# A two-layer decoder kernel: the second layer's VectorE roundings run one chain after the other, its next group's turns move up, and self attention's rough products are spread out

## What is computed

```
x = _layernorm(x + _L0_attn_ref(...))                 # a recurrence over 1024 steps
x = _layernorm(x + _L0_xattn_ref(x, ctx, ctx, mask0, ...))
x = _layernorm(x + _L0_ffn_ref(...))
x = _layernorm(x + _L1_attn_ref(x, W_qkv, W_out))     # 16 heads of 64, 1024 x 1024 scores
x = _layernorm(x + _L1_xattn_ref(x, ctx, ctx, mask1, ...))   # 16 heads of 16, 77 context rows
x = _layernorm(x + _L1_ffn_ref(x, w_gate, w_up, w_down))
```

```
scale = jnp.maximum(jnp.max(jnp.abs(xb), axis=-1, keepdims=True) / 6.0, 1e-12)
q = _GRID[jnp.searchsorted(_MID, jnp.abs(xb / scale))] * jnp.sign(xb) * scale
gate = fp4_linear(x, w_gate); y = fp4_linear(x, w_up)
h = jax.nn.silu(gate) * y                             # 704 wide
return fp4_linear(h, w_down)
```

## Time and profile before

| | |
|---|---|
| time, median of 3 runs | 2963.14 us (2959.21 to 2965.66) |
| the profiled execution | 2964.39 us |
| its span, first to last instruction | 2962.7 us |
| PE, DVE, ACT, POOL busy | 2087.9, 2176.3, 1751.9, 654.3 us |
| self attention's loops | about 1653 to 2500 us of the span |
| second layer | about 2515 us to the end |

### The profile page before, as it was taken

The page is one execution under the profiler, slowest core; times in us unless marked ns, Lnnn a source line. Parts: engine busy times, 40 slices in busy tenths (PEclk is TensorE's granted clock), DMA queues, the critical chain, the costliest instruction groups (busy, mean ns, idle before and its releaser), DMA issues. The chain is left out here.

```text
span 2962.7 us, 41501 instructions
## 1 busy us (share of the span) xinstructions
PE 2087.9 (70%) x11052; PEld 1171.3 (40%) x11052; DVE 2176.3 (73%) x10063; ACT 1751.9 (59%) x5698; POOL 654.3 (22%) x343
## 2 busy tenths in 40 slices
PE   6233655556455564655566899999999998888986
PEld 3122443344343443443344333333333333555553
DVE  5899999999999999999984455555555553276557
ACT  3678888888888888888841344444444443222231
POOL 0000000000000000000001366666666666000000
PEclk9555555565555655555555899999999998899898
DMA  5632223222223222222200000000000000210100
GB/s 124 140 94 61 55 48 66 53 52 67 48 52 67 51 53 66 53 49 65 53 4 4 4 13 17 16 7 16 16 11 12 16 11 20 73 37 14 43 8 8
DMA packets 86798, 123.55 MB, mean 42 GB/s; under 512 B 17444, under 2 KB 65224, under 8 KB 86600
## 3 DMA queue, kind: packets, MB, share of 16 engines
q1 hardware_dynamic: 86600, 121.37, 17.1%
HBM read 100.33 MB, written 21.00 MB: 41 GB/s over the span
## 5 line engine op out<-in xcount | busy, mean ns | idle before, releaser
L1505 ACT ACTIVATE mix_cand<-mix_pre,mixer_cbuf 128x32 f32<-128x32 f32 x2048 | 592.8, 289 | 167.8 <-DVE mix_pre L1435 83.6
L1502 ACT ACTIVATE mix_cand<-mix_state,mixer_cbuf 128x32 f32<-128x32 f32 x2048 | 652.7, 319 | 34.9 <-DVE mix_state L1427 4.7
L1936 DVE TENSOR_REDUCE self_tops<-self_rough 128x2 f32<-128x1024 f32 x256 | 311.7, 1217 | 411.6 <-PE self_rough L1708 411.6
L1422 DVE SCALAR_TENSOR_TENSOR mix_prod<-mixer_keys,mixer_cbuf,mix_cand 128x65 f32<-128x65 f32 x2048 | 582.1, 284 | 34.2 <-ACT mix_cand L1505 27.1
L1435 DVE SCALAR_TENSOR_TENSOR mix_pre<-mixer_keys,mix_gap,mix_state 128x32 f32<-128x32 f32 x2048 | 525.8, 257 | 27.8
L1427 DVE SCALAR_TENSOR_TENSOR mix_state<-mix_cand,mixer_cbuf 128x32 f32<-128x32 f32 x2048 | 506.9, 247 | 0.1
L1534 PE MATMUL mix_out<-all_ident,mix_state 128*128 128x128 f32 x512 | 162.0, 417 | 486.3 <-ACT mix_flat L1486 430.6
L1922 POOL TENSOR_TENSOR self_psum<-self_psum,self_prob 128x1024 f32<-128x1024 f32 x192 | 451.3, 2350 | 160.4 <-ACT self_prob L1849 151.1
L1849 ACT ACTIVATE self_prob<-self_sco 128x1024 f32<-128x1024 f32 x256 | 261.5, 1024 | 118.9 <-PE self_sco L1721 108.2
L886 POOL TENSOR_TENSOR mix_st_norm_rstd<-mix_st_norm_var,mix_half 128x2 f32<-128x2 f32 x24 | 16.7, 697 | 1318.1 <-DVE mix_st_norm_var L879 1318.1
L1534 PEld LDWEIGHTS mix_out<-all_ident,mix_state 128*128 128x128 f32 x512 | 82.6, 207 | 568.6 <-ACT mix_flat L1486 502.6
(11 more groups left out here) (386 smaller groups left out, 3257.7 us busy)
## 6 DMA issues: line engine op xcount, KB each, us to landing
mixer_keys<-k_rows SPq DMA_DIRECT2D x256, 260.0 KB, 4.9
aT_rows<-self_aT SPq DMA_DIRECT2D x32, 256.0 KB, 2.3
...
```

The lines of the kernel that those rows point to most:

```text
L1422: dve.scalar_tensor_tensor(prod[:, b, :], keys[:, h, b, s_, :], coef(NIB, h, s_, b), cand[:, b, s % 2, :], ALU.mult, ALU.mult, accum_out=g ...
L1502: act.activation(cand[:, b, (s + 1) % 2, NS:2 * NS], state[:, hp, sp_, b, :], ACT.Copy, scale=cbuf[:, h, KEEP, b, s_:s_ + 1]).then_inc(kep ...
L1505: act.activation(cand[:, b, (s + 1) % 2, 0:NS], pre[b], ACT.Tanh, scale=cbuf[:, h, BETA, b, s_:s_ + 1]).then_inc(c_ready[b], 1)
L1936: dve.tensor_reduce(tops[:, kh, t, :], rough[:, :, :], AX.X, ALU.max).then_inc(rough_taken, 1)
```

## The change

It has three parts. None removes a computation, and no buffer is added.

1. **Self attention.** The pieces of `rough_scores` move. Before, pieces 0 and 1, 3 and 4, and 5 and 6 each had only one `scores` between them. Now at least one larger product, or two `scores`, stands between two pieces, but for pieces 0 and 1, which have one `scores` and an `attend`. VectorE's first inversion stands before top 5 instead of behind it.
2. **Second layer, VectorE.** `lagging` is gone. Each norm and each rounding of a chain runs to its end before the other chain's begins, and `hidden_dve` is called for each tile: one's tile 0, two's norm1, two's tile 0, one's tile 1, two's tile 1. Only the last norm is still split, around the tops of the next group.
3. **Second layer, TensorE and ScalarE.** Both `flip1` of the next group stand before the down product of chain one's second tile, behind a new wait for chain two's `h_ready` (its bank 6 must have been read); both `queries_pe` and the first rough scores of the next group stand before chain two's second down product. The scores of chain one's first half of heads are split around chain two's rough scores. ScalarE copies both chains' turned tops before the first exponentials.

```
@@ self attention, TensorE @@
                     scores(hp, b, hf, 1)
-                    if more:
-                        rough_scores(hp + 1, of, to, 1)
                     if behind:
                         attend(hp - 1, b if hf else other, 3)
                     if more:
-                        rough_scores(hp + 1, of, to, 2)
+                        rough_scores(hp + 1, of, to, 1)
...
                         keys_queries(fills, "Q1" if hf else "K0", other)
+                    if more:
+                        rough_scores(hp + 1, of, to, 2)
                     scores(hp, b, hf, 2)
+                    scores(hp, b, hf, 3)
                     if more:
                         rough_scores(hp + 1, of, to, 3)
-                    scores(hp, b, hf, 3)
-                    if more:
-                        rough_scores(hp + 1, of, to, 4)
...
                         denominators(fills, f"DEN{hf}", hp - 1, 1 - hf)
+                    if more:
+                        rough_scores(hp + 1, of, to, 4)
                     scores(hp, b, hf, 4)
+                    scores(hp, b, hf, 5)
                     if more:
                         rough_scores(hp + 1, of, to, 5)
-                    scores(hp, b, hf, 5)
+                    attend(hp, b, 1)
                     if more:
                         rough_scores(hp + 1, of, to, 6)
-                    attend(hp, b, 1)
@@ self attention, VectorE @@
-                        for r in range(6):
+                        for r in range(5):
                             top(hp + 1, r)
                         piece(0)
+                        top(hp + 1, 5)
+                        piece(1)
                         top(hp + 1, 6)
-                        piece(1)
@@ second layer, TensorE @@
-                one.xa.rough_pe(pe, g, 0, one.norm3.var_ready)
-                two.queries_pe(pe, g)
                 one.xa.rough_pe(pe, g, 1)
-                two.xa.rough_pe(pe, g, 0, two.norm3.var_ready)
+                two.xa.rough_pe(pe, g, 0, two.norm3)
                 one.xa.turn_tops_pe(pe, g)
+                one.xa.scores_pe(pe, g, 0, (0,))
                 two.xa.rough_pe(pe, g, 1)
-                one.xa.scores_pe(pe, g, 0)
+                one.xa.scores_pe(pe, g, 0, (1,))
...
-                one.ff.turn_hidden_pe(pe, g, 1, 1, 2)
+                one.ff.turn_hidden_pe(pe, g, 1, 1, 1)
+                if more:
+                    one.flip1.pe(pe, g + 1)
+                    pe.wait_ge(two.ff.h_ready, (g + 1) * CTILES)
+                    two.flip1.pe(pe, g + 1)
                 one.ff.down_pe(pe, g, 1)
                 if more:
-                    one.flip1.pe(pe, g + 1)
-                two.ff.turn_hidden_pe(pe, g, 1, 0, 3)
+                    for c in chains:
+                        c.queries_pe(pe, g + 1)
+                two.ff.turn_hidden_pe(pe, g, 1, 0, 1)
                 two.ff.turn_hidden_pe(pe, g, 1, 1, 2)
                 if more:
-                    one.queries_pe(pe, g + 1)
+                    one.xa.rough_pe(pe, g + 1, 0, one.norm3)
                 two.ff.down_pe(pe, g, 1)
-                if more:
-                    two.flip1.pe(pe, g + 1)
@@ second layer, ScalarE @@
                 for c in chains:
                     c.xa.turn_tops_act(act, g)
-                    c.xa.scores_act(act, g, 0)
-                for c in chains:
-                    c.xa.scores_act(act, g, 1)
+                for f in range(KT):
+                    for c in chains:
+                        c.xa.scores_act(act, g, f)
@@ second layer, VectorE @@
-                lagging(last, 4, tops(one, g))
-                alone(tops(two, g))
+                top(one, g, 0)
+                for _ in range(4):
+                    next(last, None)
+                top(one, g, 1)
+                top(two, g, 0)
+                alone(last)
+                top(two, g, 1)
...
-                lagging(one.round_dve(dve, g), 7, two.round_dve(dve, g))
-                alone(next_norm(one, g))
-                lagging(one.ff.hidden_dve(dve, g), 3, second_hidden(g))
+                for c in chains:
+                    alone(c.round_dve(dve, g))
+                next_norm(one, g)
+                alone(one.ff.hidden_dve(dve, g, 0))
+                next_norm(two, g)
+                alone(two.ff.hidden_dve(dve, g, 0))
+                alone(one.ff.hidden_dve(dve, g, 1))
+                alone(two.ff.hidden_dve(dve, g, 1))
```

106 lines of the change are left out of this document (48 added, 58 removed).

## The result

| | before | changed |
|---|---|---|
| median of 4 runs each, on one chip | 2961.18 us (2956.88 to 2965.66) | 2879.79 us (2876.02 to 2882.12) |
| ratio, 95% interval | | 0.9723, 0.9705 to 0.974 |
| the profiled execution; its span | 2964.39; 2962.7 us | 2881.71; 2880.0 us |
| first to last scores of self attention | 842.8 us | 803.4 us |
| first output product of the second layer to chain one's first reciprocal | 58.1 us | 54.5 us |

The change made the kernel faster: 82.7 us between the two spans. Of these 39.4 us are self attention's, 3.6 + 30.1 + 6.2 = 39.9 us the second layer's. The other 3.4 us lie outside both (3.7 us ahead of self attention, less 0.4 us between the two), in code that was not changed, and are no effect of the change: over all profiled executions the first scores of self attention start between 1645.9 and 1653.4 us.

What follows compares the result with a forecast made beforehand. TensorE was taken to bound self attention, and handovers between engines that are not full the second layer. 2964.4 - 41 (self attention) - 34 (second layer) = 2889 us profiled, 2888 us as median; range 2875 to 2912 us.

Steps and rivals of the forecast that it cites:

- 1.23 + 0.21 + 0.18 - 0.30 = 1.32 us: Self attention, each half: three removed waits and cheaper shape changes, less dearer ones, save 1.32 of 26.73 us.
- thirty halves have the full pattern: Self attention: the saving of a half counts thirty times, 39.6 us; the last half has no rough scores.
- `piece(0)` costs nothing: Self attention, VectorE: the inversion moved before top 5 is over at 13.8 us, before piece 5 is ready at 14.9.
- the slower rival: Self attention: a later ScalarE copy of the denominators stalls VectorE at `piece(0)`, delaying top 5 and piece 6; 2981 us, chance 0.03.
- the one with remaining waits: Self attention: rough scores still wait because VectorE's inversions stand among the tops; 2905 to 2935 us, chance 0.10.
- VectorE alone: Second layer: un-overlapped chain, about 0.12 us dearer per instruction; two's first hidden tile 46.8 us after one's reciprocal (R), 6.6 earlier.
- exactly the same matmuls: Second layer, TensorE: chain two's first hidden tile to chain one's second rough scores still takes 23.4 us, so these start 6.6 earlier.
- From there to chain two's first scores: Second layer, from chain one's second rough scores: 12.7 us instead of 14.05, 1.4 us less a group.
- From there on: Second layer, from chain two's first scores to the next reciprocal: 11.7 us, as before.
- The table load is just hidden: Second layer, ScalarE: load behind both copies is covered by chain two's scores; costs up to 1.3 us at full clock.
- gains from `flip1` and queries without alternation: Second layer, first group's front: this order and the split scores save 4 us.
- The end: Second layer, last group: reciprocal to end takes 67.0 us instead of 72.8, 5.8 us less.

Runs made afterwards that it cites:

- swap6: Kernel before with one edit in self attention: attend(hp, b, 1) stands before rough piece 6 instead of behind it; 2949.62 us, ratio 0.9961.
- turns_only: Changed kernel with VectorE's norms and roundings of the second layer interleaved by `lagging` again; TensorE's and ScalarE's new orders stay; 2908.71 us, ratio 0.9826.
- preload: Changed kernel plus an unread one-column Exp on ScalarE between the copies of both chains' turned tops, moving the table load there; 2880.79 us, ratio 0.9723.
- fill1: Changed kernel plus one unread matmul at each of three TensorE waits a group, for tops and copies of turned tops; 2872.74 us, ratio 0.9715.
- fill1_preload: Changed kernel plus one unread matmul at each of three TensorE waits a group and ScalarE's unread early Exp; 2868.19 us, ratio 0.968.
- front_old: Changed kernel, but ahead of the first group chain one's turn and queries again precede chain two's turn; 2875.10 us, ratio 0.9716.
- dve_alone: Changed kernel with the second layer's TensorE and ScalarE orders of before; VectorE's new order and changed self attention stay; 2895.74 us, ratio 0.9783.
- sa_only: Kernel before with self attention alone changed; 2920.66 us, ratio 0.986.
- fill: Changed kernel plus two unread matmuls at each of three TensorE waits a group, for tops and copies of turned tops; 2874.63 us, ratio 0.9716.
- best: Changed kernel plus one unread matmul at each of three waits, the unread early Exp and the old order before the first group; 2859.76 us, ratio 0.9655.

## Why the prediction was right, and where its sizes were off

- **Self attention, 41 us forecast, 39.4 measured.** The step "1.23 + 0.21 + 0.18 - 0.30 = 1.32 us" of a half holds: 26.87 to 25.53 us between the turns, 1.34 us (one half, from its first scores to the next ones': 26.73 to 25.38). Twenty-nine such halves give 39.0 us and the first 1.65 (forecast 1.5). The step that failed is "thirty halves have the full pattern". In the last pair the products for a next pair are missing, and two pieces that rely on them as spacing now wait 1.32 us each; that costs 1.2 us where a gain of 1.3 was booked. swap6's full halves show the price of a single wait to be the 0.41 us taken from the starts, not the 0.25 us that the row books (0.31 us measured, after 0.10 for the change of shapes).
- **`piece(0)` costs nothing.** The copy comes at 12.19 us, forecast 12.2. TensorE has no wait for tops in the halves with the full pattern, so the slower rival and the one with remaining waits had no case but in the last pair.
- **VectorE alone.** The whole chain came out as costed: R + 16.7, 25.3, 46.9 and 61.5, forecast 16.7, 25.3, 46.8 and 61.4. This rests on taking an instruction that waits for the one before it as dearer than an interleaved one: 0.93 us from start to start against 0.80. The Trainium skill ("VectorE: DVE Perf Modes", section The DRAIN you can't avoid) has a semaphore behind each instruction cost nothing extra; here the trace does not agree, since the instruction that could stand there instead belongs to the other chain and starts after 0.80 us.
- **TensorE from the hidden tile to the rough scores**: "exactly the same matmuls", hence 23.4 us, and R + 70.2. They took 21.26 us, and it was R + 68.2. This is the mis-sized term, 2 us a group. The work was the same. The clock was not: 0.93 before and 1.00 after. And in the new order ScalarE's copy no longer held the down product, for which TensorE had stood 0.68 us. turns_only has the new order with the old wait of 4.07 us and takes 22.46 us at a clock of 0.92: so 0.9 us are the order's and 1.2 us are a cost of the long wait beyond its own length, paid in the clock behind it. I had taken the duration behind a long wait as if it belonged to the work alone.
- **From there to chain two's first scores** 12.0 us, forecast 12.7: the first half of the scores ran at 2.4 GHz in 1.2 us (forecast 1.9). **From there on** 12.0, forecast 11.7. Together a group saves 8.6 + 2.0 - 0.3 = 10.3 us instead of 8.0.
- **The table load is just hidden.** preload says so: moving it away gains nothing as long as the scores run at 1.2 GHz. When they run at 2.4 GHz it costs 1.3 us (fill1's second group against fill1_preload's), which is the condition and the price that the prediction had given. (fill1_preload's groups are 2.0 us shorter than fill1's in the mean because fill1's clock also fell in two of three.) The Trainium skill ("ScalarE: Activation LUTs", section What ACT_TABLE_LOAD costs) has 2.66 us for a switch, of which about 1.28 are the load; the trace agrees with the load (1.28 us) and not with the sum, since the next instruction starts 1.29 us behind the load's start.
- **The first group: 3.6 us, forecast 4, which is luck.** The step "gains from `flip1` and queries without alternation" is wrong: with that order chain one's queries start 4.1 us later, and the first reciprocal comes 7.0 us later, the latter in part perhaps by the clock (front_old). It is made good by VectorE's norm of chain one, which no longer waits for chain two's rows and ends 11.5 us behind the first product instead of some 19; dve_alone has this norm and the old order, and is 9.6 us shorter than before. The size itself is uncertain by the 2.7 us between sa_only and the kernel before, which have the same instructions there. In the later groups both norms are ready long before the turns, and the same order costs nothing.
- **The end**, 6.2 us, forecast 5.8. The wait for `two.ff.h_ready` never held TensorE.

What stays open: what exactly makes TensorE's clock fall in the stretch of rough scores and scores. It fell without a wait in front of it (fill) and in some groups of a run and not in others. With one extra matmul at each of three places it stayed up in one of three groups of fill1 and in all three of fill1_preload and of best; TensorE has the same instructions in these groups of all three kernels. So the extra work is not shown to be enough, and whether the earlier exponentials or mere timing did the rest was not taken apart.
